# Joining the ternary feed-forward and the attention of a two-layer block in one program, with one written order over the seam

## What is computed

```python
x = x + ln(recurrence(ln(x)))         # W_in, a decay from W_dt, a scan over time, W_out
x = x + ln(ffn(ln(x)))                # h = silu(x@w1q.T) * (x@w3q.T);  h @ w2q.T;  hidden width 1365
x = x + ln(attention(ln(x)))          # below
x = x + ln(moe(ln(x)))                # 8 experts, top 2, and a shared expert

def ternary_quant(w):                 # w1q, w3q, w2q
    s = mean(abs(w));  return clip(round(w / s), -1, 1) * s

def attention(x):                     # 16 query heads, 8 key/value heads, head width 128
    q, k, v = x @ q_kernel, x @ k_kernel, x @ v_kernel
    q, k = rope(rms_norm(q) * q_scale), rope(rms_norm(k) * k_scale)
    p = softmax(where(j <= i and i - j < 256, q @ k.T / sqrt(128), -inf))
    return (p @ v) @ out_kernel
```

## Time and profile before

| | |
|---|---|
| time, median of 3 runs | 2139.0 us |
| the profiled execution | 2138.97 us, of which 2136.5 us are its span |
| PE busy | 1983.1 us (93% of the span) |
| DVE busy | 1485.9 us (70%) |
| ACT busy | 1164.0 us (54%) |
| POOL busy | 748.4 us (35%) |
| mean granted clock of TensorE | 0.973 of full speed |

### The profile page before, as it was taken

How to read it: one execution, slowest core, us unless ns; L and a number is a source line. 1 busy time by engine, 2 the same in 40 slices (tenths; PEclk the granted TensorE clock), 3 DMA queues, 4 the chain that set the end, 5 groups by cost and what they waited for, 6 DMA issues and landing times. The chain is left out here.

```text
span 2136.5 us, 32819 instructions
## 1 busy us (share of the span) xinstructions
PE 1983.1 (93%) x10142; PEld 1667.6 (78%) x10142; DVE 1485.9 (70%) x3511; ACT 1164.0 (54%) x2946; POOL 748.4 (35%) x1058
## 2 busy tenths in 40 slices
PE   7999999759999999999999999868999999999996
PEld 6677787537888888888888888756878888888775
DVE  7788547657766776767767777884467887774664
ACT  6742222336666666666666666643367776673332
POOL 3441001345555555555555555640600000001442
PEclk9999999869999999999999999978999999999998
DMA  7431110262000000000000000122689898884553
GB/s 253 137 130 51 42 36 20 99 243 96 21 11 21 10 0 30 0 20 10 20 10 20 10 1 6 65 69 87 239 315 327 315 322 309 306 307 156 170 187 109
DMA packets 82292, 244.78 MB, mean 115 GB/s; under 512 B 10464, under 2 KB 11104, under 8 KB 80256
## 3 DMA queue, kind: packets, MB, share of 16 engines
q1 hardware_dynamic: 77040, 226.46, 30.7%
q0 software_dynamic: 5120, 16.78, 2.3%
HBM read 207.81 MB, written 45.61 MB: 119 GB/s over the span
## 5 line engine op out<-in xcount | busy, mean ns | idle before, releaser
L269 PE MATMUL att_ps_xt<-att_w_hi,xT_hi 128*128 128x512 f32 x512 | 206.6, 404 | 28.2 <-DVE att_w_lo L2541 12.4
L2484 POOL TENSOR_SCALAR att_pr<-att_pr,att_ri 128x384 f32<-128x384 f32 (+2 forms) x256 | 136.5, 546 | 271.4 <-DVE att_ri L2579 271.4
L269 PE MATMUL att_ps_xt<-att_w_hi,xT_lo 128*128 128x512 f32 x512 | 204.5, 399 | 0.0
L269 PE MATMUL att_ps_xt<-att_w_lo,xT_hi 128*128 128x512 f32 x512 | 204.3, 399 | 0.0
L2677 ACT ACTIVATE att_pr<-att_pr,att_nb,att_r 128x384 f32<-128x384 f32 (+2 forms) x256 | 168.0, 659 | 36.8 <-DVE att_nb L2566 36.2
L2622 ACT ACTIVATE att_qkv<-att_ps_xt 128x512 f32<-128x512 f32 x128 | 76.3, 596 | 201.2 <-PE att_ps_xt L269 192.8
L1826 POOL DMA_INDIRECT y<-moe_rows,moe_slotA x16 | 16.0, 999 | 415.0 <-DMA moe_rows<-moe_lo_f 411.9
L2669 ACT ACTIVATE att_pT_hi<-att_ps_pt 128x768 fp32r<-128x768 f32 (+2 forms) x128 | 93.7, 732 | 122.7 <-PE att_ps_e L269 120.7
L269 PEld LDWEIGHTS att_ps_xt<-att_w_hi,xT_hi 128*128 128x128 f32 x512 | 97.6, 191 | 58.8 <-POOL att_w_lo L2457 23.2
L2489 POOL TENSOR_TENSOR att_rot<-att_rot 128x384 f32<-128x384 f32 x128 | 129.2, 1009 | 17.5 <-DVE att_rot L2532 17.5
L2549 DVE TENSOR_TENSOR att_q_lo<-att_ps_xt,att_q_hi 128x256 fp32r<-128x256 f32 x128 | 54.1, 423 | 112.9 <-ACT att_k_hi L2659 112.9
(11 more groups left out here) (329 smaller groups left out, 6682.6 us busy)
## 6 DMA issues: line engine op xcount, KB each, us to landing
y<-in_moe_rt SPq DMA_DIRECT2D x59, 704.0 KB, 6.5
y<-in_moe_rt SPq DMA_DIRECT2D x39, 768.0 KB, 6.5
moe_sraw_gu<-in_moe_sgu SPq DMA_DIRECT2D x44, 512.0 KB, 3.9
moe_sraw_d<-in_moe_sd SPq DMA_DIRECT2D x44, 256.0 KB, 4.2
moe_xs<-in_zeros SPq DMA_DIRECT2D x39, 256.0 KB, 9.4
moe_lo_f<-moe_xs SPq DMA_DIRECT2D x39, 256.0 KB, 6.7
moe_rows<-moe_lo_f SPq DMA_DIRECT2D x39, 256.0 KB, 6.6
att_raw_w<-in_qkv_w SPq DMA_DIRECT2D x8, 1024.0 KB, 4.8
```

Of the source, the lines that this page charges most:

```text
L269: mm = pe.matmul(out, lhsT, rhs, start=(i == 0), stop=(i == len(terms) - 1))
L2484: pool.tensor_scalar(p, p, ri[:, j % 2, g:g + 1], 1.0, ALU.mult, ALU.mult).then_inc(s("p"), 1)
```

## The change

`layer0_phase` and `attention_phase` become one `mixers_phase` with one set of semaphores, so the barrier between them goes. Groups 1 and 2 of the feed-forward run as before (`later_groups` now stops ahead of the last group), with small pieces put in `between` their blocks: the four table multiplications, the first head's weight split. The last weight group with its norms and the first 12 steps of head 0 (`LED = 12`) are written as one list of calls for each engine, tile by tile; after it `heads` goes on at step 12. The attention's tiles are laid into the room of the feed-forward's, and its PSUM banks are the feed-forward's banks; where a tile or a bank passes from one to the other, a `first_...` function adds the wait. In the norm of the feed-forward the last scaling moves from DVE (`x_norm`) to ACT (`x_norm_act`), with a small `x_shift` on DVE. SP loads the tables and head 0's weights ahead of group 2's weights; the zero fills now stand behind the last store of the feed-forward; the attention's first x tiles are loaded after the weights of head 7.

```diff
+    def x_shift(self, dve, b, tiles=range(TPB)):
+        dve.wait_ge(self.sem("x_rstd"), TPB * b + tiles[-1] + 1)
+        dve.scalar_tensor_tensor(out=self.sh2[:, ts, :], in0=self.mv2[:, ts, 0:1], scalar=-1.0, in1=self.r2[:, ts, :], ...)
+    def x_norm_act(self, act, b, tiles=range(TPB)):
+        act.wait_ge(self.sem("x_shift"), TPB * b + tiles[-1] + 1)
+        for t in tiles:
+            act.activation(self.yt(b, t), self.xsrc(b, t), ACT.Identity, bias=self.sh2[:, t, :], scale=self.r2[:, t, :])
...
-        for g in range(1, self.groups):
-            body(g, g == self.groups - 1)
+        for g in range(1, self.groups - 1):
+            body(g)
...
-        place = {..., "wd_hi": 32, "x": 40, "wgu_hi": 72, "raw_gu": 94}
+        place = {..., "wd_hi": 32, "x": 92, "wgu_hi": 72, "raw_gu": 94}
+        att_place = {"q_hi": 0, "q_lo": 2, "rot": 4, "pr": 8, "mask": 14, ..., "raw_o": 34, "gain": 38, "tab0": 40,
+                     "raw_w": 48, "w_hi": 56, "w_lo": 64, "k_hi": 72, ..., "x": 92, "qkv": 100, "o_hi": 104}
+        ps_x, ps_rt = ps_xp[:, 0, :], ps_xp[:, 1, :]
+        ps_s, ps_e, ps_o = ps_dd, ps_t[:, 0, :], ps_t[:, 1, :]
+        ps_pt = ps_out[:].rearrange("p a (b g t) -> p (a b) g t", b=2, g=GRP)
...
-            body(0, True)
+            body(0, range(LED, NT))
             with eng.Fori(1, KVH - 1) as k:
-                body(k, False)
-            body(KVH - 1, False)
+                body(k, range(NT))
+            last_head()
+            body(KVH - 1, range(NT))
...
@@ sync @@
+            sp.wait_ge(s("ps_out"), NT)
+            sp.wait_ge(post.sem("x_normed"), NT)
+            load_w(0)
...
+            f.sp_program(sp)
+            sp.wait_ge(s("w_split"), FFN1_CHUNKS)
+            for n in range(TPB):
+                f.norm.tile_load(sp, n)
...
+            f.norm.tile_stores_done(sp)
+            for n in range(RT_TILES):
+                sp.dma_start(io["moe_xs"][P * n:P * (n + 1), :], io["zeros"]).then_inc(s("slots_clear"), 16)
+            with sp.Fori(1, KVH) as k:
...
@@ vector @@
+            def between(g, b):
+                if b in (1, 2):
+                    fold_gain(g - 1, b - 1)
+                    if g == 2:
+                        split_w(0, KD // 2 + b - 1)
...
@@ scalar @@
+            def between(g, b):
+                if g == 1 and b == 2:
+                    split_w(0)
...
@@ tensor @@
+            def first_out():
+                pe.wait_ge(f.norm.sem("xT_lo"), NT)
+                project_out(0, 0, 0)
...
+            first_project()
+            ffn_turn(1, 2)
...
-        layer0_phase(nc, io, keep)
-        attention_phase(nc, io, keep)
+        mixers_phase(nc, io, keep)
```

More of the change, by code:

```diff
@@ L462, in body @@
                         self.split_hi(act, g, b, c - 1, size)
[L463 to L466 removed]
+                between(g, b)
         self.later_groups(body)
[L469 to L475 removed]
     def times_up(self, dve, g, b, c):
@@ new lines, in _ @@
+            f.norm.x_rstd(pool, 3, (3,))
+            rope_add(7, 7)
+            rms(8, 8)
+            weigh(4, 4)
+            split_v(8, 8)
+            rope_add(8, 8)
+            rms(9, 9)
+            weigh(5, 5)
+            rope_add(9, 9)
+            split_v(9, 9)
+            split_v(10, 10)
+            rms(10, 10)
+            weigh(6, 6)
+            rope_add(10, 10)
+            rms(11, 11)
+            weigh(7, 7)
+            rope_add(11, 11)
+            weigh(8, 8)
+            heads(pool, step, last_head)
@@ L1110, in _ @@
+            split_p(6, 6)
+            rope(11, 11)
+            inverse(8, 8)
+            sum_out(5, 5, True)
+            split_e(6, 6)
+            split_qk(9, 9)
+            split_p(7, 7)
+            heads(dve, step, last_head)
         @block.scalar
@@ L1363, in _ @@
+            heads(act, step, last_head)
         @block.tensor
@@ L1588 @@
+            weigh_v(3, 3)
+            turn_p(4, 4)
+            project_out(0, 2, 2)
+            scores(6, 6)
+            weigh_v(4, 4)
+            turn_p(5, 5)
+            project_out(0, 3, 3)
+            scores(7, 7)
+            turn(9, 9)
+            weigh_v(5, 5)
+            project_out(0, 4, 4)
+            scores(8, 8)
+            turn_p(6, 6)
+            project_out(0, 5, 5)
+            weigh_v(6, 6)
+            turn_p(7, 7)
+            heads(pe, step, last_head)
 EXPERTS, I_MOE, I_SHARED = 8, 352, 1408
```

1579 lines of the change are left out of this document (1050 added, 529 removed).

## The result

The changed kernel takes 2106.7 us (median of 4 runs, 2104.56 to 2107.3), the kernel before 2139.2 (4 runs, 2136.2 to 2146.0). The ratio is 0.9845, 95% interval 0.9826 to 0.9864: faster by 32.5 us. The forecast was 2090 (2076 to 2107). The direction and the main mechanism hold, but the time lies at the range's upper end, nearer to the *DVE and POOL* rival's 2105 than to my own number: a third of the forecast gain of 49 us is missing. A second set of five runs of the same kernel gave 2106.5 us, ratio 0.9843 (0.9830 to 0.9856).

The account below looks back on a forecast made before the run. PE bounds the kernel, losing time at the seam of feed-forward and attention. Profiled 2138.97 us, less 208 - 158 = 50 for the stretch (head 93, tail 65), plus 1 for preparation: 2090 us, range 2076 to 2107.

Parts of the forecast that it names:

- DVE and POOL: Rival, chance 0.18: the two engines hinder each other after the last down product, adding 22 us to DVE; 2105 us.
- Bound and bulk of the gain: Seam of feed-forward and attention: PE waits or runs slow; 208 us falls to 158, a gain of 50; PE's work 147.
- My own signs of being wrong: Wrong if the stretch from last group's first gate product to step 12's projection exceeds 170 us, or over 3 us moves outside.
- port rival: Same rival as DVE and POOL, chance 0.18: DVE operations with two SBUF inputs wait for POOL's on a shared port; 2105 us.
- Head: Last group's first gate product to its last down product: 90 us of PE work at busy share 0.98, taken as 93.
- blocking list: Rival, chance 0.04: in-order lists with a row too early block others; stretch 223 us at 0.66, kernel 2155 us.
- Tail: Last down product to step 12's projection: 59 us of DVE at 0.885 against 57 of PE at 0.98; taken as 65.
- Groups before: Feed-forward groups 1 and 2, with table products and weight splits moved in: 0 to 3 us longer, taken as 1.
- From step 12 on: Attention from step 12 to the end: nothing reordered, register multiplication hidden; heads 1 to 7 and experts as long as before.
- Late weights of head 1: Start of head 1: forecast margin 15 us, cost nothing; as rival, chance 0.04, 10 us of PE idle gives 2100 us.
- Tight packing: Rival, chance 0.14: the list packs like the plain groups, stretch 147 / 0.99 = 148.5 us, time 2080 us.

Follow-up runs that it names:

- the best order: Changed kernel plus all order edits that gained (down tiles first, output split late, weight copies spread and others): 2095.2 us, again 2095.6; ratio 0.9798 and 0.9803 to the kernel before.

## Why the prediction was right in kind and 17 us short

- **Bound and bulk of the gain: right.** The seam was the loss, and weaving won it. PE's work in the stretch, 147 us by my count, is borne out: in the best order PE is busy for 149.5 of 157.3 us, 6.8 of them at half clock, which is 146.1 us of work at full clock.
- **My own signs of being wrong: one is met, one lies on the border.** I had named a stretch above 170 us, or a time that moves outside of it by more than 3 us. The stretch is 169.4 us in one profile and 170.7 in the other, not 150 to 166; outside of it 5.0 us went (38.7 won inside, 33.7 in the span). The clock didn't stay at 1.00 either (0.98 and 0.93, then 0.95 and 0.95). The time lies within the range because its upper end was drawn for the port rival, at 2105 us, and that rival gave only a part of the missing time: so the number is partly luck.
- **Head, forecast 93, measured 98.0 to 100.8: the step that failed first.** I took PE's busy share of another list as the rate. A rate says nothing of one row that stands in a wrong place. With it moved the head takes 89.2 us, better than my 93. The two idles (7.2 us), the low clock behind the first (1.6) and in some executions behind the second (2.7) make the difference. It was in the order lists of both kernels: the old one runs all four down tiles of a block straight behind the first chunk of the next block; the new one keeps the last two tiles back for three chunks more, until behind the first chunk of the block after that. My "blocking list" rival had this mechanism, but I priced it only for the whole stretch at once.
- **Tail, forecast 65, measured 71.4 and 70.0: the wrong reason in part.** I priced 59 us of DVE at a rate of 0.885. DVE's work was 63.7 us, and the mean, 0.89, looks like my rate; but it is made of 28.05 in the first 28.7 us (0.98) and 35.6 in the other 42.7 (0.83), where PE has 39.57 at clock 0.92. So DVE limits the first part, and in the second the clock and single waits count, for which I had no term: 6.8 to 10.2 us of the tail run at half clock, and at most half of that, 3.4 to 5.1 us, is lost work. The *DVE and POOL rival* was partly true: I had given it 22 us of DVE and +15; it has 7.8 of DVE. What they cost in time was not measured as a whole. The one large meeting that was taken away, 2.2 us, gave 0.7 in the tail.
- **Groups before: forecast 1, found about 2**, within their scatter. **From step 12 on: forecast "nothing", found 2.0 us** in the attention, and 0.9 in the experts, while all that follows the stretch scatters by 4 us from one execution to the next (1603.7 to 1607.8) and is always above the 1601.1 us of the one profile before. This term was put at nothing without a test; it is 3 to 7 us, and its cause stays open.
- **Late weights of head 1: did not happen.** Their load starts at 484.0 us, and PE's wait for the split at head 1 is 1.0 us, about as at the later heads.
- **Tight packing: did not happen** for the changed kernel, but nearly for its head once the tiles were moved (88.4 of 89.2 us busy).
- The sum by measured terms: 50 - 5 (head) - 6.4 (tail) = 38.6; less 2.0, 2.0 and 0.9 is 33.7 us of span.

## What to carry to other kernels

Price a hand-written order row by row at the places where a buffer is handed back, not by the busy share of another list: one misplaced group of down tiles cost 8 us of time, more than any other edit showed but the undoing of the weaving. Beside a nearly full engine, 6 us more of its work cost 3 to 4 us here and 4.4 us less gave 1.4, while taking away a single wait may only move it. Don't read a mean busy share over a stretch whose parts have different limits. Before crediting an edit, look whether the two profiles had the same granted clock behind the same idle: in this case that changes two gains of 2 to 3 us into 0.7 and 1.4.

## What the runs showed of the hardware

- An idle of 4.41 us of PE was followed by products at 0.43 us spacing (1.2 GHz) in all eight profiles that have it; the one of 2.77 or 2.78 us behind it was followed by full clock in four of them and by about 5.5 us at the lower level in the four others (0.66 to 0.68 over 10 us), for the same instructions.
- The same holds in the tail. In the two profiles of the same program, behind the wait of 2.2 us ahead of step 1's transposition, the granted clock over 10 us is 0.67 in one and 0.83 in the other (43 against 52 products), and the tail 71.4 against 70.0 us.
- A DVE operation of 128 x 2 elements took 0.98 us beside a POOL addition of 128 x 384 (1.01 us), where its mean is 0.18 in the quiet part: the length of the wait is that of the other's instruction, not of one's own.
- POOL's powers over 1 and 3 elements for each partition, 0.55 to 0.86 us long, did not lengthen such operations (0.34 us at 454.11, as usual). Beside POOL's scaling with one tensor input an operation of 0.28 us took 0.49 (at 439.98) and ended 0.1 us after it.
